# A window-attention block on one core: the 64 tokens of a window numbered by column instead of by row

## The reference

```python
h = layernorm(x, norm1_g, norm1_b)
# windows of 8x8 pixels: 1024 windows of N = 64 tokens, C = 48
hw = h.reshape(B, H//8, 8, W//8, 8, C).transpose(0, 1, 3, 2, 4, 5).reshape(-1, 64, C)
q, k, v = split(hw @ qkv_w + qkv_b)            # 3 heads of 16
attn = softmax(q*SCALE @ k.T + rel_bias_table[REL_IDX])
out = (attn @ v) @ proj_w + proj_b              # back to (B, H, W, C)
x = x + out
h2 = layernorm(x, norm2_g, norm2_b)
return x + gelu(h2 @ fc1_w + fc1_b) @ fc2_w + fc2_b
```

## Time and profile before

| | us |
|---|---|
| median of 3 runs | 1110.33 |
| the three runs | 1105.14, 1110.33, 1111.57 |
| the profiled execution | 1109.31 |
| its span, first to last instruction | 1107.5 |
| busy in the span: PE / PEld | 1052.1 / 924.5 |
| DVE / POOL / ACT | 800.1 / 757.8 / 710.7 |
| mean granted TensorE clock | 0.988 of full speed |

### The profile page before, as it was taken

One profiled execution on the slowest core, in us unless ns is written; L12 is line 12 of the kernel. 1 busy time (PEld: TensorE's weight loads), 2 busy tenths in 40 slices (PEclk: granted clock), 3 DMA queues, 4 the chain that ended last, 5 costly groups with the idle time before them and its releaser, 6 DMA issues.

```text
span 1107.5 us, 26440 instructions
## 1 busy us (share of the span) xinstructions
PE 1052.1 (95%) x7366; PEld 924.5 (83%) x7366; DVE 800.1 (72%) x2301; ACT 710.7 (64%) x1347; POOL 757.8 (68%) x1174
## 2 busy tenths in 40 slices
PE   2899999999999999999999999998899999999997
PEld 0688888888888888888888888887699999999997
DVE  4667767777777777677777777767477777777773
ACT  1556676666766667666666666665466766666674
POOL 5367765667655677656776667764578888888881
PEclk9989999999999999999999999999699999999999
DMA  1001110001110011100111001100011111111111
GB/s 43 27 16 36 38 36 32 28 32 41 35 35 28 28 43 34 36 28 28 43 35 37 28 28 39 35 25 15 15 29 43 43 43 43 43 43 43 40 40 48
DMA packets 24807, 38.25 MB, mean 35 GB/s; under 512 B 4119, under 2 KB 20698, under 8 KB 24794
## 3 DMA queue, kind: packets, MB, share of 16 engines
q1 hardware_dynamic: 24722, 37.90, 10.9%
q10 hardware_dynamic: 72, 0.20, 0.0%
HBM read 25.50 MB, written 12.58 MB: 34 GB/s over the span
## 4 chain that ended last, share of the span: by engine, by line
issue 34%; PE 32%; POOL 29%; DVE 2%; POOLq 1%; ACT 1%; DMA 1%; ACTq 0%; DVEq 0%
PE scores_ps L594 15%; POOL rstd L377 11%; POOL lowered L464 6%; PE x_ps L587 5%; PE x_ps L581 4%; POOL centred L373 4%; POOL normed L383 3%; PE x_ps L571 3%; PE scores_ps L539 1%; PE mixed_ps L554 1%; POOL small L365 1%; DMA x_in<-in_x 1%; POOL small L359 1%; POOL small L368 1%; POOL small L364 1%
## 5 line engine op out<-in xcount | busy, mean ns | idle before, releaser
L464 POOL TENSOR_TENSOR lowered<-biased,row_top 128x384 f32<-128x384 f32 x256 | 212.1, 829 | 264.1 <-DVE row_top L980 263.6
L787 ACT ACTIVATE probs<-lowered 128x384 f32<-128x384 f32 x256 | 134.3, 525 | 180.7 <-POOL lowered L464 179.8
L377 POOL TENSOR_TENSOR rstd<-small,minus_half 128x4 f32<-128x4 f32 (+1 forms) x160 | 242.9, 1530 | 0.0
L554 PEld LDWEIGHTS mixed_ps<-v_blocks,probs_t 128*128 128x128 f32 x1536 | 196.0, 193 | 44.7 <-ACT probs_t L768 24.4
L539 PE MATMUL scores_ps<-k_blocks,q_blocks 96*128 96x192 f32 x1024 | 225.9, 344 | 1.6 <-DVE q_blocks L968 1.6
L554 PE MATMUL mixed_ps<-v_blocks,probs_t 128*128 128x66 f32 x1536 | 209.4, 273 | 7.8 <-ACT probs_t L768 3.4
L976 DVE TENSOR_TENSOR biased<-scores_ps,pos 128x384 f32<-128x384 f32 x256 | 142.2, 555 | 83.1 <-PE scores_ps L539 79.1
L594 PEld LDWEIGHTS scores_ps<-wfc,hidden 128*128 128x128 f32 x1536 | 181.0, 192 | 6.2 <-issue 0.5
L594 PE MATMUL scores_ps<-wfc,hidden 128*128 128x96 f32 x1536 | 179.9, 274 | 0.3 <-ACT heads_t L803 0.3
L768 ACT ACTIVATE probs_t<-probs_t_ps 128x384 f32<-128x384 f32 x256 | 125.0, 488 | 82.3 <-PE probs_t_ps L546 80.4
L539 PEld LDWEIGHTS scores_ps<-k_blocks,q_blocks 96*128 96x128 f32 x1024 | 163.8, 193 | 4.3 <-DVE q_blocks L968 2.1
(11 more groups left out here) (100 smaller groups left out, 1615.1 us busy)
## 6 DMA issues: line engine op xcount, KB each, us to landing
x<-in_x SPq DMA_DIRECT2D x128, 96.0 KB
out<-x SPq DMA_DIRECT2D x128, 96.0 KB
x_in<-in_x SPq DMA_DIRECT2D x244, 48.0 KB
x_second<-in_x SPq DMA_DIRECT2D x8, 48.0 KB
x_in<-in_x ACTq DMA_DIRECT2D x4, 48.0 KB
pos_in<-in_L_conv_rel_bias_table SPq DMA_DIRECT2D x8, 10.6 KB
wproj<-in_L_conv_proj_w SPq DMA_DIRECT2D x6, 3.0 KB
wfc_in<-in_L_conv_fc_w SPq DMA_DIRECT2D x2, 36.0 KB
```

The lines of the kernel that those rows point to most:

```text
L377: pool.tensor_tensor(rstd[:, groups], small[:, 7, groups], minus_half[:, groups], ALU.pow).then_inc(step, 1)
L464: pool.tensor_tensor(lowered[:, k % 2, :, :], biased[:, k % 2, :, :], broadcast(row_top[:, k % 2, :], 2, TOK), ALU.subtract).then_inc(lowe ...
L554: mm = pe.matmul(mixed_ps[:, at:at + MIX], probs_t[:, h, :], v_blocks[:, part, u, h, :], start=True, stop=True)
L787: act.activation(probs[:, k % 2, :, :, :].rearrange("p h a t -> p a h t"), lowered[:, k % 2, :, :].rearrange("p (a h) t -> p a h t", a=2), ...
```

## The change

Within a window, the tokens are numbered j·8 + i instead of i·8 + j. Both copies on ScalarE that go between the two orders are rewritten, and so is the bias; everything between them (projections, scores, softmax, mix) is as before and only sees other numbers. The count of instructions, transfers and elements stays.

- tokens_out now reads runs of 8 elements (i) and writes runs of 8, of which the four j of a half lie side by side, 32 elements in all.
- heads_out writes as before, and reads runs of 8 elements instead of one element in 8.
- The table's transfers go over pj: their first partition index runs over the table's rows, with a step of REL = 15 elements, instead of 1. The copy into pos_all reads with an inner step of 15 elements instead of 1.

```diff
-        def token_view(tokens, half):
-            view = tokens.rearrange("c k (ai j) -> c j (k ai)", j=WIN)
-            return view[:, HALF * half:HALF * half + HALF, :]
...
-            for pi in range(WIN):
-                load(pos_in[WIN * pi:WIN * pi + WIN, :, :], bass.AP(
-                    table.tensor, REL * pi, [[1, WIN], [TABLE, HEADS], [1, REL * (WIN - 1) + WIN]]), table_in)
+            for pj in range(WIN):
+                load(pos_in[WIN * pj:WIN * pj + WIN, :, :], bass.AP(
+                    table.tensor, pj, [[REL, WIN], [TABLE, HEADS], [1, REL * (WIN - 1) + WIN]]), table_in)
...
-                      pos_all[:, :, :, :].rearrange("p h i j -> p (h i j)"), start=True, stop=True).then_inc(pos_mm, 1)
+                      pos_all[:, :, :, :].rearrange("p h j i -> p (h j i)"), start=True, stop=True).then_inc(pos_mm, 1)
...
             def tokens_out(half):
-                source = x_ps[half][0:C2, :].rearrange("c (j t) -> c j t", j=HALF)
-                act.activation(token_view(tokens_t[0:C2, :, :], half), source, ACT.Copy).then_inc(tokens_ok, 1)
+                source = x_ps[half][0:C2, :].rearrange("c (j ka i) -> c ka j i", j=HALF, i=WIN)
+                view = tokens_t[0:C2, :, :].rearrange("c k (a j i) -> c (k a) j i", a=2, j=WIN)
+                act.activation(view[:, :, HALF * half:HALF * half + HALF, :], source, ACT.Copy).then_inc(tokens_ok, 1)
...
             def heads_out(bank, part):
                 at = 2 * WIN * UNITS * part
-                act.activation(heads_t[0:C2, :, at:at + 2 * WIN * UNITS],
-                               bank[0:C2, :].rearrange("c (ubi j) -> c j ubi", j=WIN), ACT.Copy).then_inc(heads_t_ok, 1)
+                act.activation(heads_t[0:C2, :, at:at + 2 * WIN * UNITS].rearrange("c j (ua i) -> c j ua i", i=WIN),
+                               bank[0:C2, :].rearrange("c (ua j i) -> c j ua i", j=WIN, i=WIN), ACT.Copy
+                               ).then_inc(heads_t_ok, 1)
...
             wide = bass.AP(pos_in, 0, [[HEADS * (REL * (WIN - 1) + WIN), TOK], [REL * (WIN - 1) + WIN, HEADS],
-                                       [REL, WIN], [1, WIN]])
+                                       [1, WIN], [REL, WIN]])
```

## The result

The changed kernel took 1103.99 us (median of 6 runs, 1100.79 to 1107.38), the kernel before beside it 1110.95 us (6 runs, 1105.14 to 1111.75): a ratio of 0.9942, 95% interval 0.9920 to 0.9965, so about 6.4 us less. The forecast was 3.8 us and 1106.5 us.

What follows compares the result with a forecast made beforehand. It took the attention stage to be bound by TensorE's ring through ScalarE's token copies, with an x_in transfer ring beside it. Savings of 3.3 + 0.5 = 3.8 us took 1109.31 to 1105.5; the median's 1.0 more gave 1106.5 us, range 1100.5 to 1112.5.

Steps and rivals of the forecast that it cites:

- Price of the copies: Token copies on ScalarE, two per batch: 0.59 us each in place of 1.13, the step on the write side being the cost.
- The ring through the copies: TensorE's chain of waits per batch, closed through ScalarE's token copies: 0.19 us shorter, from 23.19 to 23.00 us.
- The transfer ring: Second chain per batch: VectorE's second add_proj, SP's issues, the x_in transfer, the statistics; 23.04 us, just above TensorE's new 23.00.
- the take-back of 0.08: Two nearly equal chains with about 0.2 us of scatter end about 0.08 us above the larger, so 23.12 us per batch.
- the reckoned 0.54 us: VectorE's wait for x_in from which a batch grows after the change: 0.54 us, where it was about 0.73.
- Waiting in nearly every batch: Predicted sign: VectorE's statistics wait longer for the x_in transfer, in nearly every batch.
- The start: Second token copy before the first scores: 0.59 instead of 1.08 us, and everything behind it follows, saving 0.5 us.
- the loss of the 0.19 us in the first batch: First batch: TensorE's 1.91 us wait for VectorE's heads grows by 0.19 us, so that gain is lost there.
- rival 3: TensorE's low-clock stretch, 56 to 60 us or near 780, lengthens or drops: 3.5 us either way, 1103 or 1110; chance 0.12.
- Head copies and bias: ScalarE's head copies stay 0.59 us; the bias copy into pos_all takes at most 0.34 us more, hidden: zero, at most 0.3.
- The sum: Whole kernel: 3.3 us over 30 batches plus 0.5 us before the first scores, 3.8 us saved.
- ScalarE 34 us less busy: Predicted sign: 64 token copies, each 0.54 us shorter, make ScalarE 34 us less busy.

## Why the prediction was right

- **Price of the copies.** 0.59 us forecast, 0.589 measured; the price is on the write side, as the earlier trace rows said and the two reordered copies together showed. The rule of the Trainium skill (PSUM — Partial Sum Buffer, Specifications) that spoke against the change is about matmuls and does not carry over to ScalarE's reads: with steps of 32 B and of 512 B they took 588 and 590 ns, side by side 599.
- **The ring through the copies.** 0.19 us per batch forecast from two distances between starts; with early transfers the batch went from 23.20 to 23.01. That is exact. In the changed kernel alone the usual batch shows it too (23.19 to 23.01), but the mean hides part of it.
- **The transfer ring.** Its 23.04 us and the take-back of 0.08 were sized from one wait's mean and scatter; the mean batch came out at 23.12 us in both executions, as forecast, and 23.01 with the transfers moved. The wait from which a batch grows came out at the reckoned 0.54 us, and so did the half of the batches: in the two executions 17 and 12 of 29 were lengthened. "Waiting in nearly every batch" was no sign of the change, since 27 of 29 waited already before it.
- **The start.** The 0.5 us came, and the loss of the 0.19 us in the first batch as a longer wait (by 0.25 us) came too. What I had put at nothing in the sum is the clock behind that wait, 1.7 us in the profiled pair. It was rival 3, and its price (up to 3.5 us either way) was of the right size. That the longer wait is the reason isn't shown: one kernel with the same wait of 2.17 us kept the shorter stretch.
- **Head copies and bias.** 588 ns unchanged; the bias copy 0.13 us longer and hidden.
- **The sum.** 3.8 us forecast, 4.0 measured at equal clocks (2.6 to 5.4) and 6.4 in the first measurement, whose runs had more of the higher mean clock. That the sum is so near is partly luck. Its main term was right, 3.1 us over the batches against 3.3; but in both traces of the changed kernel the first steady batch begins later than in the trace before, by 1.15 and 0.94 us, where I had 0.5 us earlier. Against that one trace the two spans are 1.8 and 2.6 us shorter, and only over all runs does it come to 4.0. "ScalarE 34 us less busy" was wrong: 24.9 by the page. I multiplied 64 copies by the difference of their means, but neighbouring instructions overlap: the pair fell by 0.97 us and not by 1.07, and the exponential behind it used to start 0.22 us before its end. The path was costed from TensorE's side and didn't use that number.

## What to carry to other kernels

Cost a shorter instruction by what waits for it, from start-to-start distances with and without the wait; then look for the second ring that is only a few hundredths shorter, because it decides how much of the gain stays, and its repair (here one semaphore count) may be worth as much again. For a copy on ScalarE, try first the order in which it goes through its elements, before changing any layout: here it was enough that the fp32 writes lay side by side in runs of 16 B. When work on an in-order engine is moved earlier, list what is queued behind the instruction it delays on the *next* engine too.

## What was not expected of the hardware

A wait of TensorE of 2.16 us, with a granted clock of 1.00 before it, was followed by some 10 us around the lower clock, and one of 1.03 us at the same place was not; with 1.1 us taken out of that wait the first steady batch began at 70.25 and not 75.41 us, 5.2 us earlier. One of 1.21 us, 9 us earlier in another kernel, was followed by a low stretch, so the length of the wait alone doesn't tell. And the stretch came in two sizes, 3.4 or 5.1 us of full-speed work, behind waits as equal as 2.16 and 2.17 us. And ScalarE pays for single fp32 writes 32 B apart (1126 and 1071 ns for 512 columns) but not for the same writes grouped by four (590 ns).
